# A graph layer on one core: 15 of its gathered tiles fetched row by row by SyncE, and four one-hot picks fewer

## The reference

```python
features = H[id_Xe[0]]                                   # a row of x for each edge's source
M_in = jnp.concatenate([features, Xe], axis=1)
Y = jax.nn.relu(M_in @ M_W.T + M_b)                      # a message for each edge
Z = jax.ops.segment_sum(Y, id_Xe[1], num_segments=H.shape[0])
U_in = jnp.concatenate([H, Z], axis=1)
H_next = jax.nn.relu(U_in @ U_W.T + U_b)
x = _layernorm(x + H_next, axis=-1)
```

## Time and profile before

| | us |
|---|---|
| median of 3 runs | 1693.86 |
| lowest, highest | 1693.01, 1695.35 |
| the profiled execution, its time | 1692.73 |
| its span in the profile | 1690.7 |
| PE busy | 1646.8 |
| DVE busy | 1342.5 |
| POOL busy | 1252.5 |
| ACT busy | 321.7 |
| granted TensorE clock, mean | 0.993 |

### The profile page before, as it was taken

The page is one execution under the profiler, slowest core; times in us unless marked ns, Lnnn a source line. Parts: engine busy times, 40 slices in busy tenths (PEclk is TensorE's granted clock), DMA queues, the critical chain, the costliest instruction groups (busy, mean ns, idle before and its releaser), DMA issues.

```text
span 1690.7 us, 42848 instructions
## 1 busy us (share of the span) xinstructions
PE 1646.8 (97%) x18500; PEld 1580.2 (93%) x18500; DVE 1342.5 (79%) x1372; ACT 321.7 (19%) x647; POOL 1252.5 (74%) x1334
## 2 busy tenths in 40 slices
PE   6899999999999999999999999999999999999995
PEld 5899999999999999999999999999999999999991
DVE  5787887888788788788788878878878878878873
ACT  4421111111111111111111111111111111111113
POOL 6777777777777777777777777777777777777763
PEclk9999999999999999999999999999999999999997
DMA  7222222222222222222222222222222222222211
GB/s 169 63 61 59 59 59 59 59 59 59 59 59 65 58 54 65 59 59 60 59 59 59 59 59 59 64 54 59 65 59 59 60 59 59 59 58 59 59 40 40
DMA packets 143890, 103.59 MB, mean 61 GB/s; under 512 B 97195, under 2 KB 121724, under 8 KB 143698
## 3 DMA queue, kind: packets, MB, share of 16 engines
q0 software_dynamic: 41920, 42.99, 13.4%
q1 hardware_dynamic: 100660, 56.18, 12.8%
q10 hardware_dynamic: 1118, 1.62, 0.4%
HBM read 97.48 MB, written 3.20 MB: 60 GB/s over the span
## 4 chain that ended last, share of the span: by engine, by line
PE 96%; DVE 1%; ACT 1%; issue 0%; DMA 0%; POOL 0%; DVEq 0%; SPq 0%; POOLq 0%; ACTq 0%
PE p_pick L901 61%; PE p_messages L908 13%; PE p_messages L870 10%; PE p_edges_T L852 7%; PE p_bc L888 3%; PE p_messages L954 1%; DMA u_stage<-in_L_gnn_U_W_dram 0%; ACT block_start L445 0%; DVE XZ L638 0%; POOL Y L389 0%; PE p_messages L809 0%; PE p_edges_T L820 0%; DVE onehot_src L693 0%; PE p_pick L784 0%; ACT Y_parts L456 0%
## 5 line engine op out<-in xcount | busy, mean ns | idle before, releaser
L362 POOL DMA_INDIRECT gathered<-Y_rows,src_all x1267 | 1195.7, 944 | 386.2 <-issue 382.8
L901 PE MATMUL p_pick<-Y_parts,onehot_src 128*128 128x192 bf16 x12397 | 1053.9, 246 | 0.4 <-DVE onehot_src L693 0.4
L901 PEld LDWEIGHTS p_pick<-Y_parts,onehot_src 128*128 128x128 bf16 x12397 | 1028.7, 98 | 11.2 <-issue 0.7
L693 DVE TENSOR_TENSOR onehot_src<-p_dve,block_start 128x6272 bf16<-128x6272 int16 x253 | 860.4, 3422 | 6.8 <-DVE p_dve L683 0.2
L471 ACT COPY edges_T<-p_edges_T 128x512 f32<-128x512 f32 x196 | 114.7, 585 | 1181.6 <-PE p_edges_T L852 1181.6
L908 PE MATMUL p_messages<-onehot,messages 128*64 128x72 f32 x3126 | 238.4, 230 | 4.4 <-ACT messages L491 4.4
L908 PEld LDWEIGHTS p_messages<-onehot,messages 128*64 128x64 f32 x3126 | 209.2, 137 | 28.2 <-ACT messages L491 5.0
L870 PE MATMUL p_messages<-w_edges,edges_T 128*128 128x128 f32 x1564 | 212.2, 279 | 3.5 <-ACT edges_T L471 3.4
L870 PEld LDWEIGHTS p_messages<-w_edges,edges_T 128*128 128x128 f32 x1564 | 190.0, 192 | 4.8 <-DVE XZ L701 2.5
L659 DVE TENSOR_REDUCE gathered<-p_pick 128x64 f32<-128x192 f32 x253 | 88.4, 349 | 98.8 <-PE p_pick L901 98.8
L650 DVE SCALAR_TENSOR_TENSOR onehot<-p_dve,base,dst_all 128x576 f32<-128x576 f32 x195 | 157.5, 808 | 0.0
(11 more groups left out here) (100 smaller groups left out, 197.3 us busy)
## 6 DMA issues: line engine op xcount, KB each, us to landing
edges<-in_edge_attr_dram SPq DMA_DIRECT2D x190, 192.0 KB
gathered<-Y_rows,src_all POOLq DMA_INDIRECT x1267
edges<-in_edge_attr_dram SPq DMA_DIRECT2D x191, 64.0 KB
Y_rows<-Y SPq DMA_DIRECT2D x6, 256.0 KB
out_dram<-Y SPq DMA_DIRECT2D x6, 256.0 KB
edges<-in_edge_attr_dram SPq DMA_DIRECT2D x5, 256.0 KB
xb<-in_x_dram SPq DMA_DIRECT2D x1, 768.0 KB
gathered<-in_x_dram,src_first POOLq DMA_INDIRECT x40
```

The source lines that it names most:

```text
L362: nc.gpsimd.indirect_dma_start(out=gathered[c % G][0:parts, j * D:(j + 1) * D], out_offset=None, in_=table, in_offset=bass.IndirectOffsetO ...
L693: nc.vector.tensor_tensor(onehot_src[k % SLOTS][:, :, :], sources.unsqueeze(1).to_broadcast([P, NW, P]), block_start[:, :, :], ALU.is_equa ...
L901: last = nc.tensor.matmul(p_pick[k % 2][:, 0:3 * D], onehot_src[k % SLOTS][:, b, :], Y_parts[:, b, :], start=(b == 0), stop=(b == NW - 1))
```

## The change

`picked_tiles` drops tile 6 of the chunks 48, 96, 144 and 192, which is gathered by POOL instead. Tile 6 of 15 other chunks (25, 37, 49, ... 193, every twelfth) is no longer gathered by POOL. SP fetches its 128 rows one by one: after the edge loads of a chunk it reads 12 node numbers from `row_sources` into registers and issues 12 DMAs of one row (256 bytes) each, with the DRAM address from a register, into `row_tile[t % 2]`. Eleven such steps (8 rows in the first, 12 in each of the others) make a tile; the last stands behind the loads of the tile's own chunk. ACT copies `row_tile` into the `gathered` buffer after it has rectified the messages of the chunk before, and DVE waits for that copy too in `add_rows`. The chunks 25, 37, ... are not among those with two picks. From chunk 5 on POOL has 1256 gathers and 3, and PE has 249 picks.

```diff
@@ -65,12 +65,23 @@
-        return [TILES - 2, TILES - 1] if c % 3 == 0 else [TILES - 1]
+        return [TILES - 2, TILES - 1] if c % 3 == 0 and c % 48 else [TILES - 1]
+
+    ROWS_TILE = TILES - 2
+    ROWS_EVERY = 12
+    ROWS_AT_ONCE = 12
+    row_chunks = [c for c in range(2 * ROWS_EVERY + 1, NC, ROWS_EVERY) if ROWS_TILE not in picked_tiles(c)]
+    row_steps = {row_chunks[t] - s: (t, P - s * ROWS_AT_ONCE - ROWS_AT_ONCE)
+                 for t in range(len(row_chunks)) for s in range(-(-P // ROWS_AT_ONCE))}
...
-        return [j for j in range(TILES) if j not in picked_tiles(c)]
+        return [j for j in range(TILES)
+                if j not in picked_tiles(c) and not (c in row_chunks and j == ROWS_TILE)]
@@ -124,6 +135,8 @@
+        row_sources = sb("row_sources", [len(row_chunks), P], i32)
+        row_tile = [sb(f"row_tile{u}", [P, D]) for u in range(2)]
@@ -335,8 +351,29 @@
+            sp.dma_start(row_sources[:, :],
+                         chunk_rows(src)[row_chunks[0]:NC:ROWS_EVERY, ROWS_TILE * P:(ROWS_TILE + 1) * P]
+                         ).then_inc(s_row_sources_loaded, 16)
+
+            def load_rows(t, r0):
+
+                r1, r0 = r0 + ROWS_AT_ONCE, max(r0, 0)
+                if t >= 2 and r0 == 0:
+
+                    sp.wait_ge(s_rows_copied, t - 1)
+                _, ends = nc.values_load_multi_w_load_instructions(
+                    row_sources[t:t + 1, r0:r1], engines=(mybir.EngineType.SP,), min_val=0, max_val=N - 1,
+                    skip_runtime_bounds_check_because="the ends of edges are nodes")
+                for r, end in zip(range(r0, r1), ends):
+                    sp.dma_start(row_tile[t % 2][r:r + 1, :], Y_rows[bass.ds(end, 1), :]).then_inc(s_rows_landed[t % 2], 16)
+
             for c in range(SLOTS, NC + 1):
                 load_edges(c)
+                if c in row_steps:
+                    if c == min(row_steps):
+                        sp.wait_ge(s_row_sources_loaded, 16)
+                        sp.wait_ge(s_Y_stored, 16 * stores)
+                    load_rows(*row_steps[c])
@@ -491,6 +528,13 @@
+            def copy_rows(c):
+
+                t = row_chunks.index(c)
+                act.wait_ge(s_rows_landed[t % 2], 16 * P * (t // 2 + 1))
+                nc.scalar.copy(gathered[c % G][:, ROWS_TILE * D:(ROWS_TILE + 1) * D], row_tile[t % 2][:, :]
+                               ).then_inc(s_rows_copied, 1)
@@ -504,6 +548,8 @@
                 rectify(c)
+                if c + 1 in row_chunks:
+                    copy_rows(c + 1)
@@ -671,6 +717,8 @@
                     dve.wait_ge(s_gathered[c % G], gathered_by(c))
+                    if c in row_chunks:
+                        dve.wait_ge(s_rows_copied, row_chunks.index(c) + 1)
```

More of the change, by code:

```diff
@@ L67, in picked_tiles @@
             return []
-        return [TILES - 2, TILES - 1] if c % 3 == 0 else [TILES - 1]
+        return [TILES - 2, TILES - 1] if c % 3 == 0 and c % 48 else [TILES - 1]
[5 more added lines that the diff above has]
+                 for t in range(len(row_chunks)) for s in range(-(-P // ROWS_AT_ONCE))}
+    assert ROWS_EVERY * ROWS_AT_ONCE >= P and len(row_chunks) == len(range(2 * ROWS_EVERY + 1, NC, ROWS_EVERY))
     def gathered_tiles(c):
@@ L242, in gnn_residual_layernorm_kernel @@
         s_gathered = [sem(f"s_gathered{u}") for u in range(G)]
+        s_row_sources_loaded = sem("s_row_sources_loaded")
+        s_rows_landed = [sem(f"s_rows_landed{u}") for u in range(2)]
+        s_rows_copied = sem("s_rows_copied")
         s_edges_T = sem("s_edges_T")
```

## The result

The median of the changed kernel is 1672.57 us over 4 runs (1671.87 to 1672.90), that of the kernel before 1693.57 over 4 runs. The ratio is 0.9876, with a 95% interval of 0.9864 to 0.9888: faster by 21.0 us. The forecast was 1676.9, its range 1674.5 to 1683.0.

What follows compares the result with a forecast made beforehand. PE was taken to bound the kernel, with POOL at the same rate and slightly ahead. Four dropped picks save 17.0 us and all else costs nothing: 1693.86 - 17.0 = 1676.9 us, range 1674.5 to 1683.

Steps and rivals of the forecast that it cites:

- PE sets the end, POOL runs at the same rate: Whole run: PE takes 25.00 us for three chunks, POOL's twenty gathers 24.98; PE ends last because POOL has a lead.
- PE saves 4 x 4.24 = 17.0 us: PE's rounds: each dropped pick saves 4.03 us in its round and 0.21 in the round before.
- the sign that the prediction named: PE rounds of 6.9 us five times in a row around chunks 48, 96, 144 and 192.
- POOL saves 11 x 1.249 and keeps a margin of 1.6 us at the last chunk: POOL's gathers: 15 leave, 4 come, 13.7 us less; lead at the last chunk falls from 4.9 to 1.6 us.
- SP: 78.6 of 98.9 us, a row 0.45, a register load 1.07: SP in twelve chunks: 9.2 us edge loads, 11.8 register loads, 57.6 rows; SP still waits, so rows cost nothing.
- The sign that SP would wait after each step: SP's queue: SP still waiting for the transposes after each step of rows.
- The threshold of 0.61 us a row: SP's row issue: SP becomes the bound if one row costs more than 0.61 us.
- The small parts at nothing: ACT's 15 row copies, DVE's added wait and the load of `row_sources` (0.3 to 0.5 us) were all costed at nothing.
- The sum: Whole run: 1692.73 - 17.0 = 1675.7 us profiled, median 1.1 us above; forecast 1693.86 - 17.0 = 1676.9 us.
- Rivals: Four: SP bound by row issue 7%; SP paying each landing 1%; POOL bound 8%, 3% and 2%; rows late 1%.
- SP as the bound: SP's row issue above 0.61 us makes PE wait for edges; 1954 us at 0.76 us a row; chance 7%.
- POOL as the bound: Gathers slowed by extra transfers: 1683.4 us at 0.5%, 1691.5 at 1%; 8% between 1679 and 1690, 3% same, 2% beyond.

Runs made afterwards that it cites:

- the picks alone: Kernel before with the four picks dropped and gathered by POOL instead, no rows by SP: 1692.23 us, ratio 0.9996.
- 15 registers a load: Changed kernel with a row tile every ninth chunk, 15 rows a step, five picks dropped, drain behind POOL's last gather: 1911.44 us, ratio 1.1297 to the kernel before.
- the two runs with all picks: Changed kernel with the old `picked_tiles`: 1690.25 us, 0.9982; kernel before without the 15 row tiles' gathers, nothing in their place: 1690.1 us, 0.9986.
- twenty rows: Changed kernel with eight more row transfers in each step, into a tile nobody reads: 1765.73 us, ratio 1.0440 to the kernel before.
- an early drain: One POOL drain right behind its last gather: 1669.51 us (0.9858) in the changed kernel, 1687.66 us (0.9970) in the kernel before.

## Why the prediction was right or wrong, point by point

- **PE sets the end, POOL runs at the same rate.** Right, and shown: the picks alone gain nothing (0.9996), and DVE then waits for gathers.
- **PE saves 4 x 4.24 = 17.0 us.** Right: 16.96 at the last chunk. The short rounds in a row are fed. Four of them take 6.9 us; the sign that the prediction named had five, but the fifth spreads two picks and takes 7.13.
- **POOL saves 11 x 1.249 and keeps a margin of 1.6 us at the last chunk.** The sign was right; 1.1 us were left, since DVE's last addition came 17.3 us earlier and not 17.0, and the last gather 13.5 and not 13.7. The gathers kept their pace: 944 ns busy and a start every 1.249 us.
- **SP: 78.6 of 98.9 us, a row 0.45, a register load 1.07.** Measured 0.41 and 0.94; with 0.80 for a pair of loads that is 9.6 + 10.3 + 52.5 = 72.4 us. Both sizes were a little high. Some 0.25 us in a step is in none of these sizes; by its waits SP has 23 us of room in a group. The sign that SP would wait after each step did not hold: it waits in 88 of the 180 chunks of the groups, since a step fills a short round. With 15 registers a load it has no room. The threshold of 0.61 us a row was not tried as such, but its sum was, from the other side: 106 us in a group gave 93 us more. That rows on SP are free is shown by the two runs with all picks, 2.7 us below the kernel before with rows and 2.4 without.
- **The small parts at nothing.** The 15 copies took 0.255 us each; no wait of ACT for rows appears. The one DMA for `row_sources` took 0.63 us.
- **The sum, the step that failed.** "1692.73 - 17.0 = 1675.7": it carried PE's saving to the end of the run as if everything behind POOL's last computation stayed as it was. It went by the chain that ended last, which ends with that computation (its last group is POOL's), and not by the rows of the program's end. There POOL's drain took 9.07 us behind the computation and now takes 6.38. Why it became shorter stays open; the runs show that leaving out gathers brings it by itself (6.30 us with 15 fewer and 6.38 with 5 fewer, all picks kept and no rows), though the length does not follow their number. The profiled executions are 1692.73 and 1672.69: 20.0 = 17.0 at the last chunk, 0.3 between that and DVE's last additions, 2.7 in the drain. A second term was off, too. The sum put the median 1.1 us above the profiled execution, as in the three runs before; with the change the median of 1672.57 is 0.1 below it. So the 4.3 us between 1676.9 and 1672.57 are 2.7 of drain, 0.3 at the last addition and 1.2 of that offset, the rest rounding. The offset came from three executions: later runs of the kernel before, 21, 15 and 10 on their chips, had medians of 1692.97, 1692.48 and 1692.73, within 0.3 us of its profiled execution. The same offset is the 1.0 us between the 20.0 of the profiled executions and the 21.0 of the medians.
- **The range.** It was built from one-sided mishaps, all of which lengthen the run. Its lower end allowed 2.4 us for everything unknown that could shorten it, less than the drain alone gave.
- **Rivals.** None of them took place. SP as the bound became real with twenty rows, by more rows and not by dearer ones, and POOL as the bound with the picks alone, by more gathers at the same pace.

## What to carry to other kernels

When two engines keep the same pace, moving work from one to the other is worth nothing (0.9996 here) until the other is relieved too, and the first number to read is the lead at the point where they meet. Idle issue time of SP or ACT can then carry small transfers that relieve the engine that gathers, as long as the steps of a group fit the rounds of the group, with the slack of the edge loads to even them out, and their register loads are whole multiples of 16 bytes (8, 12 and 16 registers were fast here, 15 were not). And read the end of the program too: POOL's drain, which outlasted the last store here, can be the last thing that is waited for, and moving it under other work costs one line.

## What the runs showed of the hardware

- POOL's drain had 3.0 to 9.2 us of work behind the gathers, most often near 3, 6.3 or 9 us. With an early drain the end drain ends 0.07 us behind the last computation. What sets the value was not settled: neither the number of gathers, nor the idle time before it, nor the row transfers explains it.
- A row of 256 bytes with its DRAM address from a register costs SP 0.41 us to issue (0.228 of it the DMA instruction), 0.31 where the address was already worked out, and ACT 0.40 (3.20 us for 8).
- A load of registers from SBUF took 0.72 us for 8, 0.94 for 12 and 1.18 for 16, but 1.57 for 15 from a multiple of 16 bytes and 3.26 from any other start.
